# Image rows 2p and 2p+1 on partition p in the mixing stage of a four-layer kernel

## The reference

```
L0: z = einsum('bikc,bkjc->bijc', a, b)            16 channels
L1: x1 = einsum('bikd,bjkd->bijd', a1, b1)         16 channels
    x2 = einsum('bkid,bkjd->bijd', a2, b2)         16 channels
L2: tri = einsum('bikc,bjkc->bijc', a, b)          64 channels
L3: out = einsum('bkid,bkjd->bijd', left, right)   64 channels
```

## Time and profile before

| | |
|---|---|
| median of 3 runs | 1943.2 us (1935.28 to 1946.1) |
| profiled execution, its own time | 1933.59 us |
| its span, first to last instruction | 1931.8 us |
| TensorE matmuls busy | 1538.0 us, 80% |
| VectorE busy | 1331.0 us, 69% |
| ScalarE (ACT) busy | 882.9 us, 46% |
| GpSimd busy | 265.5 us, 14% |
| moved by DMA | 386.36 MB, mean 200 GB/s |
| L955 loads in mix | 352 of 256 KB, 3.6 us to landing |
| L1030 stores in mix | 176 of 256 KB, 3.6 us to landing |

### The profile page before, as it was taken

The page is one execution under the profiler, slowest core; times in us unless marked ns, Lnnn a source line. Parts: engine busy times, 40 slices in busy tenths (PEclk is TensorE's granted clock), DMA queues, the critical chain, the costliest instruction groups (busy, mean ns, idle before and its releaser), DMA issues. The chain is left out here.

```text
span 1931.8 us, 29873 instructions
## 1 busy us (share of the span) xinstructions
PE 1538.0 (80%) x7296; PEld 758.3 (39%) x7296; DVE 1331.0 (69%) x2126; ACT 882.9 (46%) x1446; POOL 265.5 (14%) x224
## 2 busy tenths in 40 slices
PE   5597498966586576999979995667999967766998
PEld 4445233211275122222239992222222235652447
DVE  3884499067588696377757776993577757767994
ACT  3795343833234244766646662005666634440003
POOL 0000087000000484100000001661100000000000
PEclk8998799999898798999989997998999989997999
DMA  5667410035567440098889995870388879976759
GB/s 201 212 132 220 128 47 13 5 108 142 157 214 261 100 89 3 11 309 280 279 274 299 304 302 183 289 280 1 129 288 279 282 250 307 309 252 228 273 211 348
DMA packets 253817, 386.36 MB, mean 200 GB/s; under 512 B 24227, under 2 KB 165414, under 8 KB 244262
## 3 DMA queue, kind: packets, MB, share of 16 engines
q1 hardware_dynamic: 205718, 337.35, 54.2%
q10 hardware_dynamic: 48016, 47.98, 7.5%
HBM read 193.74 MB, written 190.32 MB: 199 GB/s over the span
## 5 line engine op out<-in xcount | busy, mean ns | idle before, releaser
L993 PE MATMUL bank<-work 128*128 128x256 f32 x1408 | 346.8, 394 | 59.0 <-ACT work L1025 31.8
L719 ACT ACTIVATE work<-bank,bias 128x512 f32<-128x512 f32 x448 | 276.9, 686 | 210.8 <-PE bank L617 135.4
L1345 POOL TENSOR_TENSOR xT<-xT,work 128x512 f32 (+1 forms) x192 | 241.9, 1270 | 846.6 <-DVE work L1399 846.5
L784 DVE SCALAR_TENSOR_TENSOR work<-bank,bias,work 128x512 f32<-128x512 f32 x320 | 228.4, 747 | 138.3 <-PE bank L650 94.7
L993 PEld LDWEIGHTS bank<-work 128*128 128x128 f32 x1408 | 265.1, 197 | 113.6 <-issue 23.2
L650 PE MATMUL bank<-work,w 64*128 64x512 f32 x1024 | 268.8, 627 | 5.4 <-DVE work L784 4.0
L1018 ACT COPY work<-bank 128x512 f32<-128x512 f32 x176 | 103.2, 586 | 230.0 <-PE bank L993 129.1
L706 ACT ACTIVATE work<-bank,fold 128x512 f32<-128x512 f32 x192 | 116.7, 689 | 190.3 <-PE bank L617 190.0
L1284 PE MATMUL bank<-work,w 128*128 128x512 f32 (+2 forms) x512 | 193.3, 612 | 1.3 <-DVE work L1362 1.3
L1273 PE MATMUL bank<-work,sel 128*128 128x512 bf16 x176 | 70.1, 403 | 151.0 <-DMA work<-rstd_parts 98.2
L1082 DVE TENSOR_TENSOR work<-work 128x512 f32<-128x512 f32 x176 | 121.2, 689 | 70.8 <-ACT work L1018 70.1
(11 more groups left out here) (131 smaller groups left out, 1834.7 us busy)
## 6 DMA issues: line engine op xcount, KB each, us to landing
work<-hidden_rows SPq DMA_DIRECT2D x352, 256.0 KB, 3.6
hidden_rows<-work SPq DMA_DIRECT2D x288, 256.0 KB, 2.2
z_rows<-work ACTq DMA_DIRECT2D x176, 256.0 KB, 3.6
work<-z_rows SPq DMA_DIRECT2D x32, 1024.0 KB
work<-gate_rows SPq DMA_DIRECT2D x32, 1024.0 KB, 4.8
work<-in_x SPq DMA_DIRECT2D x64, 256.0 KB, 3.9
hidden_rows<-work SPq DMA_DIRECT2D x128, 128.0 KB, 2.3
gate_rows<-work SPq DMA_DIRECT2D x64, 256.0 KB, 2.4
```

Source lines behind the costliest of these rows:

```text
L719: nc.scalar.activation(result(tile, column), GB[(NG * j + n) % len(GB)][:, :], ACT.Sigmoid, bias=bias(name)).then_inc(gate_sb, 1)
L784: dve.scalar_tensor_tensor(out=r, in0=VB[(NV * j + m) % len(VB)][:, :], scalar=bias(value_w), in1=r, op0=ALU.add, op1=ALU.mult).then_inc(v ...
L993: mm = pe.matmul(ZB[b % 2][:, r * N:r * N + N], a[:, kk, r * P:r * P + P], x[:, kk, :], start=(kk == 0), stop=(kk == 1))
L1345: pool.tensor_tensor(x, x, term[:, ring(j, q, TERMS), :], ALU.add).then_inc(x_sb, 1)
```

## The change

Partition p now holds image rows 2p and 2p+1. In DRAM nothing moves. The first 64 partitions take the first half of the image and the last 64 the second half, and since the two halves lie at different rows of the DRAM tensor, each load and each store becomes two DMAs of 64 partitions, with contiguous pieces of 2 KB. So there are four loads instead of two and two stores instead of one for each channel. The bytes are the same.

The even rows now form one half of an operand (first 256 columns of the buffer) and the odd rows the other. Where the index of the output or of the contraction is such a row index, the rows have to be taken in this order: TensorE reads the other side with a step of two elements (rows_of for the stationary operand of the product, inner for the block of the transpose), or VectorE writes the turned b with a step of two, so that the product reads it straight. The masks and rstd_parts follow the same layout. In make_mask of L3 the transpose and the copy of the mask vector are gone: a DMA writes two neighbouring values to each partition.

```diff
@@ make_mask
-                sp.dma_start(mask, core.ins["L1_conv_mask"].rearrange("a (h p) k -> p (a h) k", h=2)).then_inc(landed, 16)
+                sp.dma_start(mask, core.ins["L1_conv_mask"].rearrange("a (p e) k -> p (a e) k", e=2)).then_inc(landed, 16)
...
-            sp.dma_start(m2[0:2, :], m.rearrange("a (h p) -> (a h) p", h=2)).then_inc(landed, 16)
+            sp.dma_start(mcol, m.rearrange("a (p e) -> p (a e)", e=2)).then_inc(landed, 16)
...
-            pe.transpose(core.bank[0][:, 0:2], m2[0:2, :], core.ident[0:2, 0:2]).then_inc(rep, 1)
...
+            dve.wait_ge(landed, 32)
+            dve.tensor_tensor(msq, mcol, mcol, ALU.mult).then_inc(made, 1)
             dve.wait_ge(rep, 1)
-            dve.tensor_copy(mcol, core.bank[0][:, 0:2]).then_inc(made, 1)
-            dve.wait_ge(rep, 2)
-            dve.wait_ge(made, 2)
-            dve.tensor_tensor(msq, mcol, mcol, ALU.mult).then_inc(made, 1)
@@ mix
-    src = [r.rearrange("(h m) (p k) -> m p h k", h=2, k=N) for r in rows]
-    zdst = core.z_d[0:2 * cz, 0:HALF].rearrange("(h m) (p k) -> m p h k", h=2, k=N)
+    src = [r.rearrange("(h m) (u x) -> m h u x", h=2, x=2 * N) for r in rows]
+    zdst = core.z_d[0:2 * cz, 0:HALF].rearrange("(h m) (u x) -> m h u x", h=2, x=2 * N)
+    image_half = lambda h: slice(64 * h, 64 * h + 64)
...
                 for o in range(2):
-                    sp.dma_start(loaded(o, b).rearrange("p (h k) -> p h k", h=2),
-                                 src[o][ds(at[o], 1)].rearrange("m p h k -> p (m h) k")).then_inc(landed[b], 16)
+                    for h in range(2):
+                        sp.dma_start(loaded(o, b)[image_half(h), :],
+                                     src[o][ds(at[o], 1), h].rearrange("m u x -> u (m x)")).then_inc(landed[b], 16)
...
                                 mm = pe.transpose(TB[o][b % 2][:, kk * N + r * P:kk * N + r * P + P],
-                                                  x[:, r, kk * P:kk * P + P], core.ident[:, :])
+                                                  x[:, r, inner(kk)], core.ident[:, :])
...
+            def rows_of(r):
+                return slice(r * P, r * P + P) if turns[0] else slice(r, N, 2)
+
+            def inner(kk):
+                return slice(kk * P, kk * P + P) if turns[1] else slice(kk, N, 2)
...
-                        mm = pe.matmul(ZB[b % 2][:, r * N:r * N + N], a[:, kk, r * P:r * P + P], x[:, kk, :],
+                        mm = pe.matmul(ZB[b % 2][:, r * N:r * N + N], a[:, kk, rows_of(r)], x[:, kk, :],
...
-                act.dma_start(zdst[ds(at, 1)].rearrange("m p h k -> p (m h) k"),
-                              zs[:, b % 2, :].rearrange("p (h k) -> p h k", h=2)).then_inc(stored[b % 2], 16)
+                for h in range(2):
+                    act.dma_start(zdst[ds(at, 1), h].rearrange("m u x -> u (m x)"),
+                                  zs[image_half(h), b % 2, :]).then_inc(stored[b % 2], 16)
...
+                    blocks = lambda ap: ap.rearrange("q (k r p) -> q k r p", k=2, r=2)
+                    to, turned_bank = blocks(turned_to(o, b)), blocks(TB[o][b % 2][:, :])
+                    if o:
+                        to = turned_to(o, b).rearrange("q (k p r) -> q k r p", k=2, r=2)
...
-                        made = dve.tensor_copy(turned_to(o, b), TB[o][b % 2][:, :])
+                        made = dve.tensor_copy(to, turned_bank)
@@ fold_sums
-                sp.dma_start(core.rstd_d[n:n + 1, :].rearrange("a (h p k) -> p (a h) k", h=2, k=N),
-                             parts[:, n, :].rearrange("p (h k) -> p h k", h=2)).then_inc(stored, 16)
+                sp.dma_start(core.rstd_d[n:n + 1, :].rearrange("a (p x) -> p (a x)", x=2 * N),
+                             parts[:, n, :]).then_inc(stored, 16)
```

More of the change, by code:

```diff
@@ L858, in make_mask @@
         m = core.ins["L3_conv_src_mask"]
-        m2, at = core.area([P], 6000)
-        m1, at = core.area([N], at)
+        m1, at = core.area([N], 6000)
         ones, at = core.area([P], at)
@@ L954, in load @@
                 for o in range(2):
-                    sp.dma_start(loaded(o, b).rearrange("p (h k) -> p h k", h=2),
-                                 src[o][ds(at[o], 1)].rearrange("m p h k -> p (m h) k")).then_inc(landed[b], 16)
+                    for h in range(2):
+                        sp.dma_start(loaded(o, b)[image_half(h), :],
+                                     src[o][ds(at[o], 1), h].rearrange("m u x -> u (m x)")).then_inc(landed[b], 16)
             each_channel(sp.Fori, load)
             for s in stored:
-                sp.wait_ge(s, 8 * channels)
+                sp.wait_ge(s, 16 * channels)
         @block.tensor
@@ L968, in ready @@
                 else:
-                    pe.wait_ge(landed[b], (c - b) * 8 + 32)
+                    pe.wait_ge(landed[b], (c - b) * 16 + 64)
             def turn(c, b):
@@ L1015, in out @@
                 act.wait_ge(z_mm, c + 1)
-                at_least(act, stored[b % 2], 8 * (c - b % 2))
+                at_least(act, stored[b % 2], 16 * (c - b % 2))
                 at_least(act, s1_sb, c - 1)
@@ L1051, in masked @@
                 if masked_load:
-                    dve.wait_ge(landed[b], (c - b) * 8 + 32)
+                    dve.wait_ge(landed[b], (c - b) * 16 + 64)
                     for o, made in enumerate((masked_a, masked_b)):
@@ L1067, in turned @@
                     at_least(dve, z_mm, c - 1)
+                    blocks = lambda ap: ap.rearrange("q (k r p) -> q k r p", k=2, r=2)
+                    to, turned_bank = blocks(turned_to(o, b)), blocks(TB[o][b % 2][:, :])
+                    if o:
+                        to = turned_to(o, b).rearrange("q (k p r) -> q k r p", k=2, r=2)
                     if masked_turn:
-                        made = dve.tensor_tensor(turned_to(o, b), TB[o][b % 2][:, :], mask_t, ALU.mult)
+                        made = dve.tensor_tensor(to, turned_bank, blocks(mask_t), ALU.mult)
                     else:
-                        made = dve.tensor_copy(turned_to(o, b), TB[o][b % 2][:, :])
+                        made = dve.tensor_copy(to, turned_bank)
                     made.then_inc(t_sb[o], 1)
```

## The result

The changed kernel takes 1986.1 us (median of 4 runs, 1983.7 to 1990.1), the kernel before 1941.4 in the same series. The ratio is 1.0233 [1.0203, 1.0263]: slower by 45 us. The forecast said slower, 2058 us. The sign was right and the time lies inside the stated range of 1955 to 2115 us, but the forecast loss of 115 us is more than twice the measured one.

What follows compares the result with a forecast made beforehand. The prediction took DMA to bound layer 3, TensorE layer 2 and VectorE layer 1. From 1933.6 us, +108.3 for half transfers and +6.5 for edges gave 2048.4; with 9.6 from execution to median, 2058, range 1955 to 2115 us.

Steps and rivals of the forecast that it cites:

- Layer 3 is bound by DMA: Mixing in layer 3 before the change: DMA engines 0.95 busy at 305 GB/s, 321 when full; 2.45 of 2.56 us a channel.
- Halves: Mixing loads and stores: 64-partition transfers run at about half rate in either direction, 3.2 us a channel, +108.3 us together.
- upper end: Mixing: all half transfers in series at 222 GB/s, 3.5 us a channel, +160 us; 3.2 was taken nearer to this.
- Issues: Mixing queues: SP's four loads take 1.9 us a channel, ACT's two stores 0.95 us; both hidden under 3.2 us.
- edges: Start and end of each mixing call: +0.7 us for later loads, +0.6 for the last store; five calls, +6.5 us.
- Hidden, with 0.35 us left: ACT in layer 2: two store issues add 0.50 us a channel, covered by 0.85 us of free time.
- Strided reads and writes: Product weights, transposes and turned copies at every second element: 0 taken, weight loads between 0 and 117 ns each.
- The masks and rstd: Row mask: between -0.4 and +2.1 us; the 12 rstd stores: 0, at best some tenths of a microsecond each.
- the one at 2.7 us a channel: Rival in the mixing: loads and stores partly cover each other, +29.5 us with edges, giving 1973 us; chance 0.15.
- only ACT's: Rival on ACT's queue in the mixing: issues of 0.77 us each bind, +16 us in layer 2 against -23; chance 0.08.
- the 1920 and 1936 us of the other rivals: Mixing: 1920 us if halves spread over the engines, faster, chance 0.15; 1936 us if ACT's issues bind, no change, 0.08.
- VectorE's 2.07 us: VectorE in the mixing: 2 x 0.684 + 2 x 0.350 us a channel, said to allow the faster rival's 2.26.

Runs made afterwards that it cites:

- e12: The kernel before with four buffers for z and four semaphores in place of two: 1909.7 us, ratio 0.9842 to the kernel before.
- e8: The e4 kernel with ten stages added at its end that only move data, 24 DMAs of 2 KB pieces each; half loads beside half stores ran at 326 GB/s.
- e9: The changed kernel with SP's loop of loads unrolled, so that addresses are constants: 1979.6 us, ratio 1.0210 to the kernel before.
- e16: The e4 kernel with four buffers for z in place of two: 1933.1 us, ratio 0.9972 to the kernel before.
- e4: The changed kernel with whole 128-partition loads of 2 KB pieces in layers 2 and 3, stores still halves: 1976.1 us, ratio 1.0190 to the kernel before.
- e10: The e4 kernel with whole stores of z too in layers 2 and 3, finish loading z as halves: 2002.1 us, ratio 1.0321 to the kernel before.
- e11: The e10 kernel with four buffers for z in place of two: 1970.3 us, ratio 1.0162 to the kernel before.
- e1: The kernel before with each load and store cut in two by columns, on all 128 partitions, 1 KB pieces: 1938.8 us, ratio 1.0012.
- e15: The e1 kernel with four buffers for z in place of two: 1918.5 us, ratio 0.9903 to the kernel before.
- e2: The kernel before with each load and store cut in two by partitions, 64 each, 1 KB pieces: 2053.1 us, ratio 1.0599.

## Why the prediction was right or wrong

**The direction** was right, for another reason than given.

**"Layer 3 is bound by DMA"** was wrong. The share of 0.95 was taken for a limit of 321 GB/s. e12 moves the same 1 KB pieces at 362. Two more buffers took 29 us from the stretch, so the round trip of stores over two buffers held it; the 76.0 us of the earlier trace rows had named it.

***Halves*: the step that failed.** It put 3.2 us a channel on the rate, between 3.5 in series and 2.3 beside each other. The rate asks for 2.41 by e8's estimate and at most 2.61 by e9. That halves are slow "in either direction" came from the first projection, 219 GB/s when full; half stores alone run at 267 at a share of 0.91 (e8), or 293 when full. The argument for the upper end, that the two queues' shares add up, was no argument: they add up in any kernel. The measured share of 0.79 to 0.88 and the periods of 2.79 to 2.91, where the prediction wanted near 1 and near 3.2, refute it.

***Issues*: mis-sized, and the bound in layer 3.** The prediction took 4 x 0.473 = 1.9 us a channel and hid it. It used the duration of an issue as its price. Start to start it is 0.708, so 2.83, above every period of before. The trace of before had it: the two loads of one channel, in the view of L955 from 1650.7 to 1651.6, start 0.6 us apart at 0.373 us each.

```profile
L955 SPq DMA_DIRECT2D work<-hidden_rows x2: 373/373/373, 1650.8 to 1651.4; - x2
```

The same arithmetic with 0.473 + 0.23 = 0.70, or 2.8 us a channel, gives +3.9, +1.3, +6.8, +12.6 and +15.3, together +40; with the edges as predicted, 1933.6 + 40 + 6.5 + 9.6 = 1990, against 1986 measured. That the total comes this close is partly luck: what lies outside the stretches is 5.4 us short, and the 9.6 us from execution to median were 0.8 us the other way in after's.

***Issues* on ACT.** 0.35 us was to be left in layer 2. After's timeline of ACT there (start, length, idle before):

```profile
1105.20 0.59 ACT L1023 COPY work<-bank 128x512 f32<-128x512 f32 x1
1105.68 0.71 ACT L1030 ACTIVATE work<-bank,fold 128x512 f32<-128x512 f32 x1
1105.95 1.13 ACTq L1036 DMA_DIRECT2D z_rows<-work  x2
1107.26 0.59 ACT L1017 COPY work<-bank 128x512 f32<-128x512 f32 x1 [0.87 <-issue]
```

Two issues take 1.13 us, not 0.95, and the copy of the turned a starts 0.18 behind them. In 23 channels it waits for nothing but issues. With SP out of the way and four buffers (e16) this leaves layer 2 at 2.64 against 2.60, 2.5 us in all. With the two buffers that after has it leaves 2.80 (e4), as much as SP's pace takes, so of the 11.7 us that layer 2 lost neither cause can be given a part. "Hidden, with 0.35 us left" was wrong: e4 differs from e10 only in storing halves (and in finish), and has 2.80 in layer 2 where e10 has 2.60. With two buffers the halved stores cost 0.20 us a channel there, though SP is free.

***Edges*.** 11.9 us against 6.5, but the 11.9 hold all that isn't a mixing stretch. The first row mask of layer 3 starts 4.9 us after the first load's issue, before 3.5: +1.4 where +0.7 was taken.

**Right.** Strided reads and writes cost nothing that shows: a weight load of the product, now at every second element in layer 3, has a median of 197 ns there and 190 before, with the same busy time in all, 95.8 us for 95.7; TensorE is busy 10 us longer over the span, or 0.7%, and VectorE 0.5 us. e11, with VectorE's strided writes in layer 2, takes 163.8 us there, as before and e12 do, and with the strided weights 130.5 us in layer 3 for e12's 132.0. The masks and rstd show no cost that can be told apart from the edges. Of the rivals, the one at 2.7 us a channel came nearest in time (1973), by a mechanism that also isn't what happened; SP's issues were no rival at all, only ACT's. Two readings in the rivals are off: the 1920 and 1936 us of the other rivals leave out the 6.5 us of the edges, and VectorE's 2.07 us adds durations that overlap, where its busy time in layer 3 is 113.8/63 = 1.81 us a channel.

**The better version.** e12, before with four buffers for z, takes 1909.7 us, 0.9842 [0.9819, 0.9866], and beats both kernels. The new layout brings next to nothing on top: layer 3 takes 130.5 us in e11 and 132.0 in e12, and e11 pays elsewhere.

## What to carry to other kernels

Price a DMA by the distance between two starts of the issuing queue and not by the length of its issue, multiply by the DMAs of one period, and compare with the period before asking how fast the bytes move. A queue that never waits for a consumer is at its limit, whatever the busy shares say. Another limit can stand at the same height or just under it, so lift each alone and then both before giving either its part. A DMA share near 1 beside long waits for stores is not yet a bandwidth limit: try another buffer first.

## What the runs showed of the hardware

- SP's issue of a load takes 0.333 us on 128 partitions with one piece each (e1, e15), 0.373 on 128 with two 1 KB pieces (before), 0.469 on 64 with one 2 KB piece (after) and 0.599 on 64 with two 1 KB pieces (e2). Fewer partitions cost more, not less; the mechanism isn't settled here.
- With constant addresses the issue of after grew from 0.469 to 0.603 us, and the time around it fell from 0.24 to 0.07.
- 1 KB pieces on 128 partitions reach 362 GB/s in the mixing stage (e12), 2 KB pieces 366 (e11). The Trainium skill, "DMA: Bandwidth & Descriptors", Specifications, asks for 512 B for line rate; the two windows agree.
- SP's issue of a whole store took 0.333 us at first and 1.196 in the median once stores were queued behind one another (e8), while the half loads of after keep 0.469.
- Stores on 64 partitions are less slowed than loads: 267 GB/s at a share of 0.91 against 232 to 252 at 1.03 to 1.04 (e8); together with loads 326.
